# Moving the second layer's upper products of five strips from the middle stage to the scan stage

## The reference

```python
h = max(layernorm(x), 0)
D = sum(adj, axis=1); d = (D + 1e-9) ** -0.5
x = x + relu((adj * d[:, None] * d[None, :]) @ h @ W.T + b)          # layer 0
h = max(layernorm(x), 0)
h = relu(adj @ h @ gcn_w + gcn_b)                                   # layer 1
x = x + mamba(layernorm(h) * ln_g + ln_b)                           # scan over 8192 rows, 256 x 16 states
```

## Time and profile before

| | us |
|---|---|
| median of 3 runs | 2683.72 (2681.23 to 2686.16) |
| the profiled execution, device time | 2687.66 |
| its span in the profile | 2685.8 |
| TensorE busy | 2325.4 (87%) |
| VectorE busy | 2082.0 (78%) |
| ScalarE busy | 979.5 (36%) |
| GpSimd busy | 936.9 (35%) |
| moved by DMA | 643.02 MB, mean 239 GB/s |

### The profile page before, as it was taken

One profiled execution on the slowest core, in us unless ns is written; L12 is line 12 of the kernel. 1 busy time (PEld: TensorE's weight loads), 2 busy tenths in 40 slices (PEclk: granted clock), 3 DMA queues, 4 the chain that ended last, 5 costly groups with the idle time before them and its releaser, 6 DMA issues.

```text
span 2685.8 us, 22298 instructions
## 1 busy us (share of the span) xinstructions
PE 2325.4 (87%) x7072; PEld 1314.6 (49%) x7072; DVE 2082.0 (78%) x2079; ACT 979.5 (36%) x1696; POOL 936.9 (35%) x409
## 2 busy tenths in 40 slices
PE   0347688999999999999999989999999989997776
PEld 0113344444447888888885444444444444443333
DVE  5888888886645666566652599999999899999997
ACT  0000000000004555555552455555545555555552
POOL 0000000000000000000000388777778788787554
PEclk9978789999999999999999999999999999998898
DMA  8999999898766555555547655555555555551121
GB/s 337 380 398 412 394 393 388 356 404 321 263 247 236 214 214 216 197 213 196 199 183 266 231 198 210 207 208 204 198 211 213 197 207 206 204 196 63 67 75 52
DMA packets 108325, 643.02 MB, mean 239 GB/s; under 512 B 14225, under 2 KB 15025, under 8 KB 42673
## 3 DMA queue, kind: packets, MB, share of 16 engines
q1 hardware_dynamic: 92160, 604.02, 59.3%
q10 hardware_dynamic: 16048, 37.57, 4.0%
HBM read 625.28 MB, written 16.25 MB: 239 GB/s over the span
## 4 chain that ended last, share of the span: by engine, by line
PE 57%; DVE 28%; issue 8%; ACT 3%; ACTq 1%; DMA 1%; DVEq 0%; POOL 0%; SPq 0%; POOLq 0%
PE ps L813 21%; PE ps L731 13%; DVE arena L550 11%; PE ps L853 10%; DVE arena L664 6%; DVE ps L653 6%; PE ps L890 4%; PE ps L928 4%; PE ps L753 2%; ACTq L958 1%; DMA diag_h<-adj 1%; PE ps L874 1%; PE ps L909 1%; DVE ring L664 1%; PE ps L932 1%
## 5 line engine op out<-in xcount | busy, mean ns | idle before, releaser
L813 PE MATMUL ps<-adj_parts,h_parts 128*128 128x512 f32 x2592 | 593.7, 391 | 2.5 <-ACT adj_parts L1024 2.2
L442 POOL TENSOR_TENSOR rstd<-base,minus_half 128x8 f32<-128x8 f32 (+1 forms) x40 | 84.7, 2118 | 1450.7 <-DVE base L490 877.9
L853 PE MATMUL ps<-ring,diag_h 128*128 128x512 f32 x1152 | 549.0, 611 | 0.3 <-DVE arena L640 0.2
L458 POOL TENSOR_TENSOR arena<-arena 128x1024 f32<-128x1024 f32 x192 | 458.5, 2394 | 251.1 <-ACT state L1091 251.1
L813 PEld LDWEIGHTS ps<-adj_parts,h_parts 128*128 128x128 f32 x2592 | 485.0, 188 | 108.6 <-ACT adj_parts L1024 4.7
L550 DVE TENSOR_TENSOR arena<-arena,ring 128x2048 f32<-128x2048 f32 x208 | 476.8, 2292 | 67.0 <-DMA ring<-adj 49.2
L731 PE MATMUL ps<-ring,arena 128*128 128x512 f32 x928 | 437.7, 633 | 62.4 <-DMA ring<-adj 62.4
L664 DVE TENSOR_TENSOR_SCAN arena<-arena,state,ps 128x512 f32<-128x512 f32 x384 | 470.6, 1267 | 26.1 <-DVE ps L653 1.0
L853 PEld LDWEIGHTS ps<-ring,diag_h 128*128 128x128 f32 x1152 | 223.8, 196 | 252.4 <-issue 249.3
L1099 ACT ACTIVATE arena<-arena,a_sb 128x512 f32<-128x512 f32 x512 | 338.3, 708 | 0.4
L577 DVE TENSOR_TENSOR adj_parts<-ring,adj_parts 128x1024 fp32r<-128x1024 f32 x216 | 264.0, 1224 | 94.3 <-ACT adj_parts L1024 83.5
(11 more groups left out here) (85 smaller groups left out, 1783.1 us busy)
## 6 DMA issues: line engine op xcount, KB each, us to landing
ring<-adj SPq DMA_DIRECT2D x480, 1024.0 KB, 6.5
arena<-c_scratch SPq DMA_DIRECT2D x128, 512.0 KB, 3.8
diag_h<-adj SPq DMA_DIRECT2D x32, 1024.0 KB, 12.2
arena<-x ACTq DMA_DIRECT2D x16, 512.0 KB, 4.7
x_scratch<-arena ACTq DMA_DIRECT2D x8, 512.0 KB, 3.0
arena<-x_scratch ACTq DMA_DIRECT2D x16, 256.0 KB, 4.3
out<-arena ACTq DMA_DIRECT2D x16, 256.0 KB, 3.0
lower_scratch<-arena ACTq DMA_DIRECT2D x7, 512.0 KB, 2.6
```

What stands on the lines that cost most here:

```text
L458: nc.gpsimd.tensor_tensor(buf, buf, c_row, ALU.mult).then_inc(mult_done, 1)
L813: last = nc.tensor.matmul(acc[:, c, :], h_parts[:, blk % 2, layer, h_part, a * F:(a + 1) * F], adj_parts[:, buf, adj_part, c * MM:(c + 1) ...
L853: last = nc.tensor.matmul((acc_c if i else y_ps)[:, c, :], tile_of(h1, JT * s + a), blk[:, a * STRIP + c * MM:a * STRIP + (c + 1) * MM], s ...
```

## The change

Strips 2 to 6 no longer make layer 1's upper products in the middle stage. Strip 6's four blocks and strips 5 to 2's 56 blocks make layer 0 alone there, with the h0 parts alone. In the scan stage strips 2 to 7 read all 32 blocks instead of 4(i + 1), so 60 blocks are loaded a second time, and their 240 matmuls join the evenly spread list. Their sums no longer pass through DRAM: VectorE copies acc_c into s1. Strips 1 and 0 stay as they were. What before waited for layer 1's part of a piece now waits for the piece.

```diff
@@ -64,6 +64,8 @@
+DEFERRED = 2
+
@@ -103,7 +105,7 @@
-    rows_of = {i: list(range(BPS * (i + 1))) for i in range(NS)}
+    rows_of = {i: list(range(BPS * (i + 1) if i < DEFERRED else NB)) for i in range(NS)}
@@ -132,12 +134,14 @@
         if phase == "B" and i < NS - 2:
             pieces += JT
             pieces_at[q] = pieces
+            h_parts_made += 2 if i < DEFERRED else 1
+            h_parts_at.append(h_parts_made)
@@ -566,9 +570,9 @@
-                    s = loads[q][2]
-                    dve.wait_ge(h_hi_ready, 2 * (blk + 1))
-                    for layer, h in enumerate((h0, h1)):
+                    _, i, s = loads[q]
+                    dve.wait_ge(h_hi_ready, h_parts_at[blk])
+                    for layer, h in enumerate((h0, h1) if i < DEFERRED else (h0,)):
@@ -582,7 +586,12 @@
-                    dve.wait_ge(layer0_sum, n)
+                    if i == NS - 2:
+                        dve.wait_ge(blocks_done, blocks_at[load_at["B", i, BPS * (i + 1)]])
+                    elif i >= DEFERRED:
+                        dve.wait_ge(pieces_done, pieces_at[load_at["B", i, BPS * (i + 1)]])
+                    else:
+                        dve.wait_ge(layer0_sum, DEFERRED - i)
@@ -635,7 +644,7 @@
                     dve.wait_ge(blocks_done, blocks_at[load_at["C", i, rows_of[i][-1]]])
-                    if i < NS - 1:
+                    if i < DEFERRED:
                         dve.wait_ge(l1_back[i % 2], 16 * (i // 2 + 1))
@@ -793,15 +802,9 @@
             firsts = list(reversed(range(BPS * (NS - 1), NB)))
-            for layer, acc, h in ((0, acc0[NS % 2], h0), (1, acc1, h1)):
-                if layer:
-                    pe.wait_ge(normed, NS + 1)
-                for s in firsts:
-                    last = product(acc, h, s, arrived(load_at["B", NS - 2, s]), s == firsts[0], s == firsts[-1])
-                    if layer:
-                        last.then_inc(blocks_done, 1)
-                if layer == 0:
-                    last.then_inc(layer0_sum, 1)
+            for s in firsts:
+                product(acc0[NS % 2], h0, s, arrived(load_at["B", NS - 2, s]), s == firsts[0], s == firsts[-1])\
+                    .then_inc(blocks_done, 1)
@@ -825,14 +828,16 @@
                     pe.wait_ge(hi_ready, r + 1)
-                    pe.wait_ge(h_lo_ready, 2 * (r // JT + 1))
+                    pe.wait_ge(h_lo_ready, h_parts_at[r // JT])
                     last = split_product(acc0[i % 2], r, a, 0, start, stop)
-                    if stop:
-                        last.then_inc(layer0_sum, 1)
-                    if start:
-
-                        pe.wait_ge(l1_staged, n)
-                    split_product(acc1, r, a, 1, start, stop).then_inc(pieces_done, 1)
+                    if i < DEFERRED:
+                        if stop:
+                            last.then_inc(layer0_sum, 1)
+                        if start and i < DEFERRED - 1:
+
+                            pe.wait_ge(l1_staged, DEFERRED - 1 - i)
+                        last = split_product(acc1, r, a, 1, start, stop)
+                    last.then_inc(pieces_done, 1)
@@ -1063,17 +1065,17 @@
-                    if m == (1 if n == 1 else 0):
-                        move_layer1(n - 1, i + 1)
+                    if m == 0 and i + 1 < DEFERRED:
+                        move_layer1(i + 1)
@@ -1100,7 +1102,7 @@
-                for i in range(NS - 1):
+                for i in range(DEFERRED):
                     if max(handover[i] - 2, FIRST_SLOT) == g:
```

More of the change, by code:

```diff
@@ L132, in build @@
     assert adds == NS * adds_per_strip
-    pieces_at = {}
-    pieces = 0
+    pieces_at, h_parts_at = {}, []
+    pieces = h_parts_made = 0
     for q, (phase, i, _) in enumerate(loads):
@@ L1043, in layer1_input, with move_layer1 @@
                     load_l0(m)
[L1045 to L1053, removed]
+            def move_layer1(i):
+                moved = DEFERRED - 1 - i
+                act.wait_ge(pieces_done, pieces_at[load_at["B", i, BPS * (i + 1)]])
+                if moved:
+                    act.wait_ge(l1_out, 16 * moved)
                 nc.scalar.activation(halves(l1_stage), acc1, ACT.Copy).then_inc(l1_staged, 1)
-                act.wait_ge(l1_staged, n + 1)
+                act.wait_ge(l1_staged, moved + 1)
                 act.dma_start(upper1_dram[:, i * STRIP:(i + 1) * STRIP], l1_stage).then_inc(l1_out, 16)
@@ L1064, in _ @@
                     r += 1
-                    if m == (1 if n == 1 else 0):
-                        move_layer1(n - 1, i + 1)
+                    if m == 0 and i + 1 < DEFERRED:
+                        move_layer1(i + 1)
                     if m == 7:
                         layer1_input(n)
-            move_layer1(NS - 2, 0)
+            move_layer1(0)
             layer1_input(NS - 1)
@@ L1075, in _ @@
                 act.wait_ge(x1_out[b], 16 * NS // 2)
-            act.wait_ge(l1_out, 16 * (NS - 1))
+            act.wait_ge(l1_out, 16 * DEFERRED)
             act.wait_ge(w_done, NS)
```

## The result

The changed kernel takes 2695.13 us (2693.33 to 2696.89, 5 runs) against 2683.72 (2681.23 to 2686.16, 5 runs): 11.4 us more, a ratio of 1.0043 (95% interval 1.0028 to 1.0057). It is slower, as forecast, and lies inside the range, but the loss is a third of the 36 us that were forecast. Its profiled execution has a span of 2692.1 us.

What follows compares the result with a forecast made beforehand. The prediction took TensorE to bound the middle stage, and TensorE and VectorE by turns the scan stage. Middle stage -92 us and scan stage +128 us made +36 on the median of 2683.7, so 2720 us, range 2670 to 2800.

Steps and rivals of the forecast that it cites:

- a ring of two buffers: Middle stage: ScalarE refills a buffer only when its products are finished, so one turn of 3.5 us sets the block.
- the middle stage's gain of 92 us: Middle stage: the changed part takes 238 us instead of 330, 199 for blocks and 39 for strip heads.
- The bound of each stage: TensorE limits the middle stage; TensorE and VectorE limit the slots by turns before, TensorE in every part after.
- A block takes 3.5 us ... I take 3.55: Middle stage, strips 5 to 2: time of one block, taken as 3.55 us, 199 us for 56 blocks.
- 9.7 us a strip: Middle stage: extra time at each strip's head, for completion steps, waits, normalisation and change of strip; 39 us for four.
- I take 5.12 us: Scan stage, 205 slots: time of a slot after the change, against 4.58 before, 111 us more.
- bound of 5.00 for the full clock: Scan stage: lower bound of a slot's time, TensorE at full clock and without modelled ends; a loss of 104 us.
- 17.5 us outright: The 19 slots before slot 0: TensorE is full there, so 0.92 us more a slot is added in full.
- B: Rival: VectorE's demand alone sets the middle stage's block, 2.6 us, scan stage absorbs all it can; 2640 us, chance 0.12.
- C: Rival: idle moments in the middle stage lower TensorE's clock; at a mean of 0.83, 8 us in all; chance 0.06.
- D: Rival: the scan stage hides none of the added work, 5.57 us a slot or the bare 206; 2798 to 2813, chance 0.12.
- E: Rival: TensorE has half its time to spare in the scan stage and takes the products for nothing; 2592, chance 0.02.

Runs made afterwards that it cites:

- e1: The changed kernel without any upper layer 1 products of strips 2 to 6 in the scan stage: 2583.05 us, ratio 0.9624.
- e2: The kernel before with the change's scan stage, so upper layer 1 products of strips 2 to 6 are added twice: 2795.54 us, ratio 1.0415.
- e3: The changed kernel with a third buffer for the high and low parts of a piece in strips 5 to 2: 2666.33 us, ratio 0.9937.
- e7: The changed kernel with layer 0's products of strips 5 to 2 as plain float32 matmuls instead of split ones, two buffers kept: 2669.30 us, ratio 0.9947.
- e6: The changed kernel with its 784 plain products spread by the room TensorE has in each slot instead of evenly: 2714.02 us, ratio 1.0117.
- e9: The kernel before with plain products spread by TensorE's room in each slot, 1.7 in each slot before slot 0: 2650.00 us, ratio 0.9879.

## Why the forecast was right in kind and wrong in size

The prediction had the mechanism in both stages: the halves are independent (e1, e2), a ring of two buffers sets the block (e3), and TensorE ends last in the slots. The step that failed is the size of two terms of its sum, which the sum subtracts from each other: a slot of 5.12 us (111 us), which measured 5.06 (97.6), and the middle stage's gain of 92 us, which measured 100.4.

**The bound of each stage** was read correctly: TensorE in the middle stage, both engines by turns in the slots, TensorE alone after the change.

**"A block takes 3.5 us ... I take 3.55"**: 3.45 measured. That the ring and no engine sets it is shown by e3. The rounding up from 3.52 worked out to 3.55 taken, and the excess over 3.45, are 5.6 of the 8.4 us by which **the middle stage's 92** fell short of 100.4. The rest is in the heads and the changes of strip: the stretch lasted 229.6 us (799.25 to 1028.81), which less 56 x 3.45 is 36.4 instead of 39.

**"9.7 us a strip"**: strip 4 took 50.75 us from one product with W to the next, less 12 x 3.45 leaves 9.35, and strips 5, 3 and 2 leave 9.6, 8.8 and 9.9 in the same way (the last with six products of strip 1's layer 1); e7 gave 30.1 us back for four, beside blocks of the same length and the four products with W that stay. Right.

**"I take 5.12 us" a slot** is the term that was mis-sized most. Measured 5.06: 97.6 us instead of 111. I had built it on TensorE's demand of 4.22 us at a clock of 0.97 and added 0.92; TensorE's busy time a slot is now 4.98, not 5.14. Most of this difference of 0.16 us is, by an estimate, the clock. In the slots of before it stands at 1.00 and, in 14 drops, at 0.50, for 54.6 of the 939 us together; a plain product steps by 0.43 us at the one and by 0.85 us at the other. TensorE was busy in 51 of the 54.6 us, so half of that, 26 us, was time lost to the clock. In the change it is 3.4 us at 0.50, 1.7 lost. The difference is 24 us, 0.12 us a slot. Nine of the 14 drops of before stand beside the wait of L949 for VectorE's addition, where TensorE had stood still for 2.3 to 2.9 us, and the other five beside waits of L874 of 2.3 to 3.2 us; in the change that wait is 0.9 us in 11 of 12 cases, and the only drop in the slots stands beside the twelfth, of 2.2 us. The prediction reads only the 41.6 us of the earlier trace rows and not this wait. Its bound of 5.00 for the full clock was nearer than the value that I chose. **"17.5 us outright"** in the lead-in: 17.6.

Both errors have the same sign, 8.4 us in the middle stage and 13.0 in the scan stage, and they sit in a difference of two terms of 100 us: 36 became 14.8, the tail's -1.9 not counted. An error of 8% in the one and 11% in the other makes 60% of their difference. From 14.8 to the spans' 6.3 it is the tail and the reading stage (-1.9 and -6.6). The execution of before that was profiled lay 4 us above its median and that of the change 1.2 below, so that the medians differ by 11.4. That is the lesson in the arithmetic, and the range, made from the bounds, was the honest number.

**The rivals.** B failed: nothing came near a block of 2.9 us with two buffers, but with a third (e3) the block is 2.72, and the result is then on B's side, 2666. C: the mean clock of the stretch fell to 0.98 only. No run shows a stretch that is at 0.50 as a whole; only for such a one would C lie above the range, and its 0.05 there had no case. The ring's own idle moments did not lower it: from 975 to 1017 us, blocks with TensorE busy 40.3 of 42 us, it is 1.00. It fell to 0.50 three times, for 3.4 us each (from 821.6, 859.2 and 903.5 us on), each time in or right behind a head, where TensorE had waited for 2.60, 2.60 and 1.35 us. The rival's direction, a lower clock beside more idle time, is what e6 shows: 0.88 in its lead-in, with TensorE 81% busy, and 1.00 in its slots, with 98.6%. D failed: TensorE is 98.5% busy, and half of the added work was hidden (e2). E failed: the slots got longer, with weight loads busy 490 of 1037 us, 47%, and the matmuls 1021.6, so the low share of the loads was no room.

**Still open:** why the slots stay at 4.48 us (e9) when TensorE's busy time is 4.24 and VectorE's 4.19 a slot. The list of waits names the largest part of TensorE's 48 idle us, the same wait for the shared accumulator as before (L976 and L700 here), and 11 of the 12 moments in these slots in which the clock was at 0.50, 47.8 of 918 us together, stand beside it. The row behind it is the window after one such wait:

```profile
PE ps L976 <- DVE arena L700: 32.2, 12, 2.9
```

```profile
1622.00:1626.00 4.00, 3.80 (x5) 1.84 (x6) 3.64 (x4) 3.60 (x5) 0.00 (x0) 0.50 0.17 72
```

No run takes this wait away, with a second accumulator or another order, so what it costs is not shown.

## What to carry to other kernels

When work is moved out of a stage whose engine is full, ask for the loop that the engines close through their buffers: here, with two buffers, it and not the next busiest engine was the next limit, and one buffer more gave 28.8 us beside the 100 of the stage's gain. When two engines take turns at being last, spreading the filling work by the room in each step (33.5 us, e9 against before) was worth more here than moving work between stages (17 us with the third buffer, e3), and after it the exchange between the stages was about one for one. A forecast that is a small difference of two large terms deserves its range and not its point.

## What had not been expected of the hardware

With TensorE filled from 92% to 98.5% its granted clock over the slots was 1.00 instead of 0.97 (e1 and e2 show the same two values), and the added work cost less than its own length: 2281 matmul records in 865.6 us busy before, 2726 in 1021.6 now, 0.351 us each for 445 more, where the plain ones alone step by 0.43. Of these 35 us the estimate above puts 24 down to the clock. The rest may be modelled ends that now overlap the next matmul, which no run shows by itself.

The clock did not follow the mean busy share alone. In the slots of before, with TensorE 92% busy, all 14 drops to 0.50 stand beside a single wait of 2.3 to 3.2 us, as the one drop in the slots of the change does beside one of 2.2 us. Such a wait did not always bring a drop: two of 2.3 and 2.9 us in the slots of before went without one, and in strip 2 of the change the wait of 2.60 us up to 973.26 did too, with 1.00 from 970 to 1017 us, where TensorE was 91% busy.
